# Merged tiles of a graph kernel: source one-hots of four windows by one 512-element comparison

## The chip, the cores and the metric

The kernel runs on one core of a Trainium2 chip. The metric is the device time of one execution in microseconds (us). A core has a matmul engine (TensorE, "PE" in the profile, its weight loads "PEld"), a vector engine (VectorE, "DVE"), an activation engine (ScalarE, "ACT"), GpSimd ("POOL") and SyncE ("SP"), which issues DMAs. Each engine works through its own instruction list and waits on semaphores.

## The reference

Two graph layers over 12,500 nodes of 64 features and 400,000 edges sorted by destination, each followed by a residual sum and a layer normalisation:

```python
# layer 0
gauss = exp(sum(-0.5 * (attr[:, None] - mu) ** 2 / (EPS + sigma ** 2), -1))      # E x 3
msg   = einsum('eko,ek->eo', (x[src] @ g).reshape(E, 3, 64), gauss)
out   = segment_sum(msg, dst) / max(cnt, 1) + x @ root_w + bias
x     = layernorm(x + silu(out + x))
# layer 1, twice a mean over neighbours
h = relu(x @ W_self1 + mean_of(x[src], dst) @ W_neigh1 + b1)
x = layernorm(x + h @ W_self2 + mean_of(h[src], dst) @ W_neigh2 + b2)
```

The two means of layer 1 are computed as dense products with a matrix of counts: how many edges run from node a to node b.

## The kernel before

Nodes lie in 98 tiles of 128. The kernel has five stretches: preparation of tables; a loop over the 98 tiles ("the tile loop"); a short check of the counts; layer 0's output; and the two dense products with the count matrix.

One turn of the tile loop does two things that share the engines.

**Counts.** For one tile of destinations it builds its 128 x 12,544 block of the count matrix in 32 windows of four destinations. Each window is a matmul of a source one-hot (128 edges x 128, which of 128 places within a tile of nodes the source has, the stationary operand) with a companion one-hot (128 edges x 392, which of 98 tiles and which of the window's four nodes, plus four columns of ones, the moving operand). Windows go in units of two: `n` = 0 to 15 is the unit, `w` = 0, 1 the window in it, `j = 2 * n + w`. VectorE writes the one-hots into a ring in SBUF (the tile `rE` in the trace), raises `a_pair` once per unit; TensorE waits for it, multiplies into PSUM (`pu`, three pairs of banks, `pw` in the trace) and raises `a_used`; ScalarE copies the unit's counts out (line 584), and raises `a_evac`. VectorE may write a ring place again only when `a_used` has passed the unit that read it.

There are three kinds of tile. A *paired* tile takes one or two pairs of edge batches per window; VectorE writes two interleaved source one-hots by one `tensor_tensor` of 256 elements (line 1281) and two companions by `tensor_scalar` (line 1283). A *merged* tile has all its window's edges in one batch of 128; per window VectorE writes one source one-hot (line 1410, `tensor_scalar`, 128 elements, the key from `parts[:, 1, j]`, one value per partition) and one companion (line 1411, `tensor_scalar`, 392 elements). The order is: two first tiles, then 40 tiles in which 26 merged and 14 paired tiles (two pairs per window) alternate, as merged, paired, merged; then 32 paired tiles (one pair per window); then 24 merged tiles. So there are 50 merged tiles and 1,600 instructions of line 1410.

**Messages.** For the same turn's 4,096 edges, POOL gathers the source rows by 32 indirect DMAs (line 498), into a buffer of two turns; ScalarE (line 545) and VectorE (line 1326) scale them by the three weights; per chunk `u` of four, VectorE compares destinations (lines 1340 and 1343), TensorE multiplies (line 809, eight f32 matmuls per destination tile that the chunk touches) and VectorE adds the sums (line 1263). In VectorE's list, `prepare` of chunk u stands behind unit 4u + 1; in TensorE's list, `chunk` does too. POOL may gather into a part of its buffer when ScalarE (`a_wg`) and VectorE (`a_wgd`) are done with it, and ends each turn with a wait for its own last gathers.

At the start of a merged tile VectorE copies the 64 integer keys `parts_i` to f32 `parts` (line 1399), loads its table words into registers (line 1316) and goes on with unit 0. After unit 1 it works off what is left of the previous tile (`listed`, lines 1268, 1276, 1474, 1439).

Of the kernel before, what the change touches and what calls it, by code (L numbers as in the profile page):

```python
# [7 lines left out]
F16 = mybir.dt.float16  # L8
BF16 = mybir.dt.bfloat16
ALU = mybir.AluOpType  # L10
# [3 lines left out]
P = 128  # L14
# [9 lines left out]
JW = P // W  # L24
NU = JW // 2
RU = 4
# [5 lines left out]
CW = HP * W  # L32
# [33 lines left out]
def gnn_kernel(nc, x, src, dst, attr, g, mu, sigma, root_w, bias, w_self1, w_neigh1, b1,  # L66
# [18 lines left out]
    with ExitStack() as ctx:  # L85
        def sb(name, shape, dt=F32):
            return ctx.enter_context(nc.sbuf_tensor(name, shape, dt))
# [8 lines left out]
        rE = sb("rE", [P, RE])  # L96
# [9 lines left out]
        comp = rE[:, o:o + RU * 4 * CW // 2].bitcast(F16).rearrange("p (r b c) -> p r b c", r=2 * RU, b=2)  # L106
        o_lo = o + RU * 4 * CW // 2
        lo1h = rE[:, o_lo:o_lo + RU * 4 * P // 2].bitcast(F16).rearrange("p (r c b) -> p r c b", r=2 * RU, b=2)
        lo_flat = rE[:, o_lo:o_lo + RU * 4 * P // 2].bitcast(F16).rearrange("p (r w c) -> p r w c", r=2 * RU, w=2)
        assert o_lo + RU * 4 * P // 2 <= RE  # L110
        o_src = 2 * KB * D
        o_dst = o
# [66 lines left out]
        consts = sb("consts", [P, 4, K * A])  # L179
        iota = sb("iota", [P, P])  # L180
        iota_2 = sb("iota_2", [P, P, 2], F16)
        iota_h = sb("iota_h", [P, P], F16)
        iperm = sb("iperm", [P, GW], F16)
        pidx = sb("pidx", [P, 1])
        ident = sb("ident", [P, P])
# [32 lines left out]
        both, behind2, merged_i, parts_i, parts = sca, bmx, winw, wi, wf  # L218
# [5 lines left out]
        pu = [pw[0], pw[1], pw[3]]  # L224
# [478 lines left out]
        def _(pe):  # L703
# [117 lines left out]
            def unit(t, n, pairs_w):  # L821

                evacuated(t, n)
                pe.wait_ge(a_pair, t * NU + (n + 1))
                for w in range(2):
                    if pairs_w == 0:
                        r = 2 * n % (2 * RU)
                        ins = pe.matmul(pu[n % 3][:, w, 0:CW], lo_flat[:, r, w, :], comp[:, r, w, :], start=True, stop=True)  # L828
                        if n % (NU // U) == 2 and w == 0:
                            ins.then_inc(a_chunk, 1)  # L830
                    for p in range(pairs_w):
                        r = ((2 * n + w) * pairs_w + p) % (2 * RU)
                        for b in range(2):
                            ins = pe.matmul(pu[n % 3][:, w, 0:CW], lo1h[:, r, :, b], comp[:, r, b, :],  # L834
                                            start=(p == b == 0), stop=(p == pairs_w - 1 and b == 1))
                            if n % (NU // U) == 2 and w == p == b == 0:
                                ins.then_inc(a_chunk, 1)
                ins.then_inc(a_used, 1)
# [75 lines left out]
            for part, (base, n) in enumerate(PARTS):  # L914
                with pe.Fori(0, tiles[n], 1):
                    pe.wait_ge(f_tab, pe.snap(fixed, min_val=16, max_val=16 * NT + 16))
                    pe.sem_inc(s_tick[0], 1)
                    with pe.Fori(0, wins, 1) as c:
                        w = nc.s_assert_within(pe.snap(c - wins + JW, min_val=0, max_val=JW - 1), 0, JW - 1,
                                               skip_runtime_bounds_check_because="the last windows of a tile")  # L920
# [91 lines left out]
        def _(dve):  # L1012
# [7 lines left out]
            V = nc.vector  # L1020
# [74 lines left out]
            behind = scan(rowa, rowb, NT, slice(0, 1))  # L1095
# [43 lines left out]
            for c in range(2):  # L1139
                V.tensor_copy(sca[0:NT, c, :], pb[6 + c][0:NT, 0:JW])  # L1140
                ins = V.tensor_copy(hist[0:NT, c, :], pb[6 + c][0:NT, 0:JW])
# [81 lines left out]
                    evacuate(dve, n, s_evv)  # L1223

            dve.wait_ge(s_tabw, 1)
            V.tensor_copy(iota_h[:], iota[:])
            V.tensor_scalar(win_p[:], iota[:, 0:JW], float(GW * P), None, ALU.mult)
            V.memset(comp[:].rearrange("p r b c -> p (r b) c")[:, :, GW:CW], 1.0)
            V.memset(gr[:], -1.0e6)
# [164 lines left out]
            def merged_counts(q, t, s=None, behind=2, following=None):  # L1394

                other = slot_of(q + 1) if s is None else 1 - s
                s = slot_of(q) if s is None else s
                dve.wait_ge(a_pair, q * NU)
                V.tensor_copy(parts[:], parts_i[:]).then_inc(a_hand, 1)
                words_of(q, s)  # L1400
                dve.wait_ge(a_hand, q + (1 - DT))
                for u in range(U):
                    for n in range(u * NU // U, (u + 1) * NU // U):

                        free = n + 1 if behind < 2 else max(n + 1, min(n + 3, 4))
                        dve.wait_ge(a_used, q * NU + free)
                        r = 2 * n % (2 * RU)
                        for w in range(2):
                            j = 2 * n + w
                            V.tensor_scalar(lo_flat[:, r, w, :], iota_h[:], parts[:, 1, j:j + 1], None, ALU.is_equal)  # L1410
                            ins = V.tensor_scalar(comp[:, r, w, 0:GW], iperm[:], parts[:, 0, j:j + 1], None, ALU.is_equal)  # L1411
                        ins.then_inc(a_pair, 1)
                        if n == 1:

                            listed(q - 1, other)
                            base_of(q, t)
                        if n % (NU // U) == 1:
                            prepare(q, s, u)
                        if following is not None:
                            merge_between(n, q, following, other)  # L1420
                for k in range(2):
                    dve.reg_mov(xw[k], words[T_X + k])
                dve.reg_mov(xn, words[T_XT])
# [357 lines left out]
```

## Time and profile before

| what | us |
|---|---|
| median of three runs | 8616.2 |
| lowest, highest | 8571.03, 8632.65 |
| span of the profiled execution, first to last instruction | 7138.9 |
| PE busy in it | 4916.9 (69%) |
| DVE busy | 4364.6 (61%) |
| POOL busy | 3409.5 (48%) |
| ACT busy | 2701.0 (38%) |

The page gives no other time for the profiled execution than its span. The three runs lie 1432 to 1494 us above that span: this is time outside the first and last instruction of the program, which the trace does not show. Busy time counts instructions of the engines and not those of their sequencers (register loads, waits). On VectorE consecutive instructions overlap: an instruction starts before the one ahead of it ends, so that a mean duration is longer than the time the instruction takes from its list.

### The profile page before, as it was taken

To read this page: it belongs to the slowest core of one execution; us is meant where nothing else is said; L and a number is where in the kernel's file an instruction comes from. 1 tells how busy PE (TensorE), PEld (TensorE's weight loads), DVE (VectorE), ACT (ScalarE), POOL (GpSimd) and SP (SyncE) were. 2 spreads that over 40 slices of the span, in tenths; PEclk is the share of its full clock that TensorE was granted. 3 is DMA by queue.
4 is the path that set the end of the run, shared out by engine and by line. 5 is a ranking of instruction groups with operands and counts; after the bars stand their busy time and mean duration, and the time that the engine had idled before them with its cause. 6 is when DMAs were issued, how large, how long until landed. Compare 5 with 4: busy or idle time off the path is not lost.

```text
span 7138.9 us, 141917 instructions
## 1 busy us (share of the span) xinstructions
PE 4916.9 (69%) x35195; PEld 3933.0 (55%) x35196; DVE 4364.6 (61%) x15089; ACT 2701.0 (38%) x8318; POOL 3409.5 (48%) x3146
## 2 busy tenths in 40 slices
PE   1466666666666655566666665565647999999999
PEld 1123444444444433444444444444437999999999
DVE  5667787777777776777777766666645222222222
ACT  3112554554555543455554455555532000000000
POOL 5013776677766665677777777777720000000000
PEclk5556888888888887788888878888867999999999
DMA  3001222222222222222222222222234999999998
GB/s 77 30 25 48 92 83 92 82 97 97 78 95 78 96 78 72 94 96 96 95 77 96 95 97 87 91 94 97 96 92 157 382 380 383 380 368 385 384 385 341
DMA packets 258332, 1082.60 MB, mean 152 GB/s; under 512 B 140102, under 2 KB 144230, under 8 KB 194406
## 3 DMA queue, kind: packets, MB, share of 16 engines
q1 hardware_dynamic: 139588, 965.46, 34.6%
q0 software_dynamic: 100352, 102.96, 6.4%
q10 hardware_dynamic: 18120, 11.31, 0.7%
q8 instruction: 78, 1.28, 0.1%
q14 instruction: 194, 1.59, 0.1%
HBM read 751.67 MB, written 327.81 MB: 151 GB/s over the span
## 4 chain that ended last, share of the span: by engine, by line
PE 39%; DVE 19%; issue 14%; POOL 11%; DVEq 10%; ACT 4%; DMA 2%; ACTq 0%; SPq 0%; POOLq 0%
PE pw L983 22%; POOL rE L498 11%; PE pw L809 9%; DVE rE L1283 5%; PE pw L834 3%; DVEq L1316 3%; DVEq L1492 2%; DVE rE L1343 2%; PE pw L781 2%; DVE rE L1281 2%; ACT rE L545 2%; DVE rE L1411 1%; ACT rB L584 1%; DMA rE<-in_x,idx 1%; DVEq L1268 1%
## 5 line engine op out<-in xcount | busy, mean ns | idle before, releaser
L498 POOL DMA_INDIRECT rE<-in_x,idx x3136 | 3407.4, 1087 | 1828.5 <-issue 1745.6
L809 PE MATMUL pw<-rE 128*128 128x193 f32 x7824 | 1688.3, 377 | 863.1 <-DVE rE L1343 810.2
L584 ACT CAST rB<-pw 128x792 bf16<-128x792 f32 x1568 | 1257.2, 813 | 2509.8 <-PE pw L834 1151.1
L809 PEld LDWEIGHTS pw<-rE 128*128 128x128 f32 x7824 | 1539.5, 222 | 1064.5 <-DVE rE L1343 985.5
L545 ACT ACTIVATE rE<-rE,cols 128x64 f32<-128x64 f32 x4704 | 1255.4, 345 | 8.1 <-DMA tab<-tab_d 8.1
L834 PE MATMUL pw<-rE 128*128 128x396 f16 x3840 | 809.8, 358 | 487.1 <-DVE rE L1283 440.6
L1283 DVE TENSOR_SCALAR rE<-iperm,gr 128x392 f16<-128x392 f16 x3840 | 1051.3, 313 | 0.1
L834 PEld LDWEIGHTS pw<-rE 128*128 128x128 f16 x3840 | 370.1, 103 | 865.9 <-DVE rE L1283 532.0
L983 PE MATMUL pw<-rB,rA 128*128 128x192 bf16 x9604 | 810.7, 246 | 0.1
L983 PE MATMUL pw<-rE,rA 128*128 128x192 bf16 x9604 | 810.5, 246 | 0.1
L983 PEld LDWEIGHTS pw<-rB,rA 128*128 128x128 bf16 x9604 | 790.7, 98 | 1.6
L983 PEld LDWEIGHTS pw<-rE,rA 128*128 128x128 bf16 x9604 | 790.5, 98 | 1.6 <-issue 0.2
L678 ACT COPY gcol<-pw 128x128 f32<-128x128 f32 x196 | 52.0, 265 | 1492.5 <-PE pw L991 1491.5
L828 PE MATMUL pw<-rE 128*128 128x396 f16 x1600 | 375.7, 353 | 329.8 <-ACT rB L584 182.2
L1343 DVE TENSOR_TENSOR rE<-iota,local 128x1024 f32<-128x1024 f32 x489 | 592.5, 1212 | 0.0
L1281 DVE TENSOR_TENSOR rE<-iota,lr 128x256 f16<-128x256 f16 x1920 | 539.2, 281 | 68.2 <-PE pw L834 24.0
L1411 DVE TENSOR_SCALAR rE<-iperm,wf 128x392 f16<-128x392 f16 x1600 | 541.0, 338 | 0.0
L1410 DVE TENSOR_SCALAR rE<-iota_h,wf 128x128 f16<-128x128 f16 x1600 | 398.3, 249 | 177.4 <-issue 149.2
L781 PE MATMUL pw<-rE 128*128 x822 | 305.9, 477 | 224.4 <-DVE rE L1276 132.6
L1263 DVE TENSOR_TENSOR rA<-pw,rA 128x193 f32 x491 | 172.4, 351 | 410.1 <-PE pw L809 409.2
L828 PEld LDWEIGHTS pw<-rE 128*128 128x128 f16 x1600 | 135.4, 99 | 510.8 <-DVE rE L1411 244.2
L1326 DVE TENSOR_TENSOR rE<-rE,cols 128x768 f32 (+1 forms) x392 | 371.4, 947 | 54.7 <-DVE wbase L1434 43.2
(258 smaller groups left out, 2550.8 us busy)
## 6 DMA issues: line engine op xcount, KB each, us to landing
rA<-count SPq DMA_DIRECT2D x392, 1568.0 KB, 8.4
count<-rB SPq DMA_DIRECT2D x98, 3136.0 KB
rE<-in_x,idx POOLq DMA_INDIRECT x3136
cols<-cols_d SPq DMA_DIRECT2D x98, 64.0 KB
cols_d<-rA SPq DMA_DIRECT2D x3, 1568.0 KB, 5.2
rA<-in_edge_attr ACTq DMA_DIRECT2D x1, 4608.0 KB
out<-gcol ACTq DMA_DIRECT2D x97, 32.0 KB, 5.7
count<-rB SPq DMA_DIRECT2D x8, 224.0 KB, 2.0
```

The source lines that it names most:

```text
L498: pool.indirect_dma_start(out=gath[:, s, u * CB + b, :], out_offset=None, in_=x, in_offset=bass.IndirectOffsetOnAxis(ap=idx[:, s, u * CB + ...
L545: ins = act.activation(wgath[:, u % 2, b, k * D:(k + 1) * D], gath[:, s, bb, :], ACT.Copy, scale=cols[:, s, 1 + k, bb:bb + 1])
L584: act.copy(stage[:, s, :, j * 2 * W:(j + 1) * 2 * W].rearrange("p h (w n) -> p w h n", w=2), pu[j % 3][:, :, 0:CW].rearrange("p w (h n) -> ...
L781: ins = pe.matmul(bank[:, 0:CW], lo1h[:, bass.ds(r, 1), :, b].rearrange("p o c -> p (o c)"), comp[:, bass.ds(r, 1), b, :].rearrange("p o c ...
L809: ins = pe.matmul(sums[side][:, 0:AW], onehot[:, side, bb, :], wgath[:, side, bb, :], start=(bb == 0), stop=(bb == CB - 1))
L828: ins = pe.matmul(pu[n % 3][:, w, 0:CW], lo_flat[:, r, w, :], comp[:, r, w, :], start=True, stop=True)
L834: ins = pe.matmul(pu[n % 3][:, w, 0:CW], lo1h[:, r, :, b], comp[:, r, b, :], start=(p == b == 0), stop=(p == pairs_w - 1 and b == 1))
L983: ins = pe.matmul(pb[s][:, 0:TW], ring[:, s, hi, :], table[:, hi].rearrange("p c d -> p (c d)"), start=False, stop=False, skip_group_check ...
L1281: V.tensor_tensor(lo1h[:, r], iota_2[:], lr[:, None, bass.ds(even, 2)].broadcast_to([P, P, 2]), ALU.is_equal)
L1283: ins = V.tensor_scalar(comp[:, r, h, 0:GW], iperm[:], float(GW * j), gr[:, bass.ds(at + h, 1)], ALU.add, ALU.is_equal)
L1343: V.tensor_tensor(onehot[:, side], iota[:, None, :].broadcast_to([P, CB, P]), local[:, :, None].broadcast_to([P, CB, P]), ALU.is_equal).th ...
L1411: ins = V.tensor_scalar(comp[:, r, w, 0:GW], iperm[:], parts[:, 0, j:j + 1], None, ALU.is_equal)
```

## The change

The source one-hots of two units, that is four windows or sixteen nodes, are written by one `tensor_tensor` comparison of 512 elements instead of four `tensor_scalar` of 128. Its first operand is a constant ramp `iota_4`, each number four times; its second is `lo_key`, the f16 keys of four windows, repeated 128 times. The four one-hots then lie interleaved, and TensorE reads its stationary operand with a step of four elements instead of one. A copy of 32 keys to f16 at the start of each merged tile is added. Since the comparison of an even unit writes the places of the next unit too, an even unit waits for one more unit of TensorE.

```diff
-        lo_flat = rE[:, o_lo:o_lo + RU * 4 * P // 2].bitcast(F16).rearrange("p (r w c) -> p r w c", r=2 * RU, w=2)
+        lo_four = rE[:, o_lo:o_lo + RU * 4 * P // 2].bitcast(F16).rearrange("p (h r c w) -> p h r c w", h=2, r=2, w=4)
...
-        iota_h = sb("iota_h", [P, P], F16)
+        iota_4 = sb("iota_4", [P, P, 4], F16)
+        lo_key = sb("lo_key", [P, JW], F16)
...
-                        ins = pe.matmul(pu[n % 3][:, w, 0:CW], lo_flat[:, r, w, :], comp[:, r, w, :], start=True, stop=True)
+                        ins = pe.matmul(pu[n % 3][:, w, 0:CW], lo_four[:, r // 4, 0, :, n % 2 * 2 + w], comp[:, r, w, :], start=True, stop=True)
...
-            V.tensor_copy(iota_h[:], iota[:])
+            V.tensor_copy(iota_4[:], iota[:, :, None].broadcast_to([P, P, 4]))
...
+                V.tensor_copy(lo_key[:], parts_i[:, 1, :])
                 V.tensor_copy(parts[:], parts_i[:]).then_inc(a_hand, 1)
...
-                        free = n + 1 if behind < 2 else max(n + 1, min(n + 3, 4))
+                        free = n + 2 - n % 2 if behind < 2 else max(n + 2 - n % 2, min(n + 3, 4))
                         dve.wait_ge(a_used, q * NU + free)
                         r = 2 * n % (2 * RU)
+                        if n % 2 == 0:
+                            V.tensor_tensor(lo_four[:, r // 4, 0], iota_4[:],
+                                            lo_key[:, None, 2 * n:2 * n + 4].broadcast_to([P, P, 4]), ALU.is_equal)
                         for w in range(2):
                             j = 2 * n + w
-                            V.tensor_scalar(lo_flat[:, r, w, :], iota_h[:], parts[:, 1, j:j + 1], None, ALU.is_equal)
                             ins = V.tensor_scalar(comp[:, r, w, 0:GW], iperm[:], parts[:, 0, j:j + 1], None, ALU.is_equal)
                         ins.then_inc(a_pair, 1)
```

VectorE's list at the start of a merged tile, before the change: the key copy (`wf` is `parts`, `wi` is `parts_i`), the load of the table words, and units 0 and 1.

```order
L1399 CAST wf<-wi 128x64
L1314 ISA
L1316 TENSOR_LOAD tab
L1401 REGISTER_ALU
L1406 REGISTER_ALU
L1410 TENSOR_SCALAR rE<-iota_h,wf 128x128
L1411 TENSOR_SCALAR rE<-iperm,wf 128x392
L1410 TENSOR_SCALAR rE<-iota_h,wf 128x128
L1411 TENSOR_SCALAR rE<-iperm,wf 128x392
L1406 REGISTER_ALU
```

The same place after the change, units 0 and 1 in full:

```order
L1400 CAST lo_key<-wi 128x32
L1401 CAST wf<-wi 128x64
L1315 ISA
L1317 TENSOR_LOAD tab
L1403 REGISTER_ALU
L1408 REGISTER_ALU
L1411 TENSOR_TENSOR rE<-iota,lo_key 128x512
L1415 TENSOR_SCALAR rE<-iperm,wf 128x392 x2
L1408 REGISTER_ALU
L1415 TENSOR_SCALAR rE<-iperm,wf 128x392 x2
```

For two units there were eight comparisons, and there are five; the piece of before shows the first four of the eight. Nothing else moves on any engine, and TensorE's list has the same instructions as before.

## Rows read from the trace of the kernel before

**Rows 1.** Busy time by stretch: stretch, its length, busy us of each engine with its count
```profile
core 0: us, PE busy (x) PEld busy (x) DVE busy (x) ACT busy (x) POOL busy (x), PEclk, DMA share, GB/s
...
620.00:2610.00 1990.00, 1227.41 (x5875) 844.80 (x5873) 1547.54 (x5632) 1037.41 (x3389) 1364.06 (x1270) 0.86 0.26 88
2610.00:4160.00 1550.00, 973.75 (x4605) 688.03 (x4605) 1166.31 (x4046) 755.39 (x2085) 1096.67 (x990) 0.81 0.26 89
4160.00:5270.00 1110.00, 667.61 (x3041) 507.80 (x3040) 720.04 (x2403) 639.11 (x2260) 788.10 (x749) 0.82 0.29 93
```

**Rows 2.** Chain that ended last, shares by line, stretches 620:2780 and then 4160:5270
```profile
by line: issue 18.1%; PE pw L809 14.8%; DVE rE L1283 10.5%; PE pw L834 6.9%; DVE rE L1281 4.8%; DVEq L1316 4.2%; DVE rE L1411 4.0%; DVEq L1492 4.0%; ACT rE L545 3.4%; DVE rE L1343 3.4%; DVE rE L1410 2.5%; ACT rB L584 2.4%; DVE rE L1326 2.0%
...
by line: POOL rE L498 50.4%; issue 23.3%; PE pw L809 7.5%; DMA rE<-in_x,idx 4.1%; ACT rE L545 1.7%; DVE rE L1343 1.6%; DVEq L1316 1.5%; PE pw L828 1.2%; DVE rE L1411 1.2%; ACT rB L584 1.1%; DVE rE L1410 0.9%; ACT sca L561 0.6%; DVE rE L1326
```

**Rows 3.** POOL's gathers: stretches 2610:4160, 4160:5270 (busy us, mean ns | idle before, releasers)
```profile
L498 POOL DMA_INDIRECT rE<-in_x,idx x990 | 1096.8, 1108 | 453.6 <-issue 429.8 <-ACT rE L545 16.8 <-DVE rE L1326 6.9
...
L498 POOL DMA_INDIRECT rE<-in_x,idx x749 | 788.1, 1052 | 290.9 <-issue 284.9 <-ACT rE L545 6.0
```

**Rows 4.** Timeline of POOL in a merged tile: start us, us, instruction [idle before]
```profile
4222.24 0.94 POOL L498 DMA_INDIRECT rE<-in_x,idx  x1 [0.30 <-issue]
4223.49 1.02 POOL L498 DMA_INDIRECT rE<-in_x,idx  x1 [0.30 <-issue]
4227.71 1.01 POOL L498 DMA_INDIRECT rE<-in_x,idx  x1 [3.20 <-issue]
```

**Rows 5.** Timeline of DVE, merged tile at 4217
```profile
4217.36 0.23 DVE L1410 TENSOR_SCALAR rE<-iota_h,wf 128x128 f16<-128x128 f16 x1
4217.52 0.31 DVE L1411 TENSOR_SCALAR rE<-iperm,wf 128x392 f16<-128x392 f16 x1
4217.75 0.24 DVE L1410 TENSOR_SCALAR rE<-iota_h,wf 128x128 f16<-128x128 f16 x1
4217.91 0.31 DVE L1411 TENSOR_SCALAR rE<-iperm,wf 128x392 f16<-128x392 f16 x1
4218.14 0.24 DVE L1410 TENSOR_SCALAR rE<-iota_h,wf 128x128 f16<-128x128 f16 x1
```

**Rows 6.** Timeline of DVE: `tensor_tensor` of 1024 f32 and 256 f16 elements, paired tile
```profile
3998.82 1.21 DVE L1343 TENSOR_TENSOR rE<-iota,local 128x1024 f32<-128x1024 f32 x1
3999.95 0.28 DVE L1281 TENSOR_TENSOR rE<-iota,lr 128x256 f16<-128x256 f16 x1
4000.15 0.54 DVE L1283 TENSOR_SCALAR rE<-iperm,gr 128x392 f16<-128x392 f16 x2
4000.62 0.28 DVE L1281 TENSOR_TENSOR rE<-iota,lr 128x256 f16<-128x256 f16 x1
```

**Rows 7.** DVE's groups on the page: busy, mean ns | idle before, releaser
```profile
L1410 DVE TENSOR_SCALAR rE<-iota_h,wf 128x128 f16<-128x128 f16 x1600 | 398.3, 249 | 177.4 <-issue 149.2
```

**Rows 8.** DVE's waits in 987:2569: us in total, times, longest us
```profile
DVE rA L1263 <- PE pw L809: 123.9, 29, 8.4
DVE rE L1410 <- issue: 60.6, 16, 5.0
DVE rB L1474 <- ACT rB L584: 30.4, 18, 2.6
DVE rB L1474 <- PE pw L781: 19.8, 14, 2.3
DVE rE L1281 <- PE pw L834: 19.7, 12, 3.7
...
DVE rE L1410 <- PE pw L828: 4.7, 5, 1.7
```

**Rows 9.** Weight loads of merged and paired tiles: duration ns min/median/max, first and last start
```profile
L828 PEld LDWEIGHTS pw<-rE x1600: 95/97/152, 685.5 to 5262.2; 128*128 128x128 f16 x178
...
L834 PEld LDWEIGHTS pw<-rE x3840: 96/98/152, 627.4 to 4149.0; 128*128 128x128 f16 x192
```

**Rows 10.** Timeline of PE behind a string of four units
```profile
4218.03 1.17 PE L828 MATMUL pw<-rE 128*128 128x396 f16 x6
4219.52 0.51 PE L828 MATMUL pw<-rE 128*128 128x396 f16 x2 [0.31 <-ACT rB L584]
4221.18 0.59 PE L809 MATMUL pw<-rE 128*128 128x193 f32 x2 [1.15 <-DVE rE L1343]
```

## Prediction

> **What bounds the kernel now.** I first split the span by stretch [rows 1], then read the chain that ended last over the stretches that hold merged tiles [rows 2]. POOL issues 32 gathers per tile, so the counts of the first view give the tiles: 1270 / 32 = 40 tiles from 620 to 2610 us (26 merged, 14 paired), 990 / 32 = 31 from 2610 to 4160, 749 / 32 = 24 from 4160 to 5270. A tile takes 1990 / 40 = 49.8 us, 1550 / 32 = 48.4 us and 1110 / 24 = 46.3 us.
>
> In the last of these, the reader should see that the chain is POOL and its gaps: 50.4% and a part of the 23.3% "issue", while line 1410 has 0.9% [rows 2]. The timeline of POOL says why: a gather is followed by a gap of 0.30 us, and once per tile by 3.20 us for the gathers' own landing [rows 4]. With the mean of 1052 ns [rows 3], a tile needs 32 x (1.052 + 0.30) + 2.9 = 46.2 us. That is the whole 46.3 us: the 24 last merged tiles go at POOL's pace, and VectorE is busy for only 720 of 1110 us.
>
> In the mixed stretch, POOL by the same sum needs 32 x (1364.06 / 1270 + 0.30) + 2.9 = 46.9 us of the 49.8 us, so it has 2.9 us a tile to spare. POOL isn't among the lines of that chain; VectorE and TensorE alternate in it, VectorE with 1547.54 us busy of 1990 [rows 1, 2]. Only here, and in the last two tiles, when the gathers are over, can VectorE's time become kernel time.
>
> **The change part by part.** *What is removed.* A mean duration is not what an instruction costs, since they overlap; the distance of starts is. In a string of a merged tile, line 1411 starts 0.16 us after line 1410, and the next 1410 starts 0.23 us after 1411 [rows 5]. So a source one-hot takes 0.16 us of the list and not its mean 249 ns [rows 7]. Four of them take 0.65 us (4 x 0.162, as 0.39 us a window less 0.23).
>
> *What is added.* The trace has no 512-element f16 comparison. It has two neighbours: 1024 f32 elements take 1.13 us from start to start (3998.82 to 3999.95) and 256 f16 elements, broadcast in runs of two, take 0.20 us [rows 6]. With half the time per f16 element, 1024 s + f = 1.13 and 128 s + f = 0.20 give s = 1.04 ns and a fixed part f = 0.07 us; 512 f16 elements then take 0.33 us. The bound above, at the f32 pace, is 0.07 + 0.53 = 0.60 us. The bound below is the 0.20 us of the 256 elements. I take 0.33: the new operand is the form of line 1281 with runs of four in place of two.
>
> So two units save 0.65 - 0.33 = 0.31 us (bounds 0.05 and 0.45), a tile 8 x 0.31 = 2.5 us, 50 tiles 125 us of VectorE's list.
>
> The Trainium skill ("VectorE: DVE Perf Modes", the tier table and the table of errata-adjusted cycles) speaks against this change: `tensor_scalar` on 16-bit data runs at four elements a cycle, `tensor_tensor` at two, and both have the same fixed 58 cycles. By its figures, an estimate, four of 128 elements cost 375 ns and one of 512 costs 327 ns, which would leave 0.4 us a tile. The row disagrees on the first term: 0.16 us and not 94 ns. The measurement decides, and the small `tensor_scalar` is mostly fixed cost.
>
> *Which of it is on the path.* Mixed stretch: 26 x 2.5 = 65 us at most. The chain bounds it from the other side: line 1410 holds 2.5% of 2160 us = 54 us there and 0.9% of 1110 = 10 us later [rows 2]; of these 64 us the fraction 0.31 / 0.65 goes, 31 us. Between the two lies what other engines absorb: VectorE already waits for engines that don't wait for it, 30.4 + 19.8 + 19.7 + 4.7 = 75 us in 1582 us [rows 8], 2.3 us a tile, and when VectorE gets faster such a wait grows. The 123.9 us for line 809 are another matter: this TensorE work starts from VectorE's own line 1343 and moves with it. I take about two thirds of 65, 42 us. The last two tiles give 2 x 2.5 less a wait, 3 us.
>
> *The POOL-bound stretch.* Nothing of the 60 us saved on VectorE counts directly. But gathers are slower while VectorE works on its strings: undisturbed 0.94 us [rows 4], in the merged stretch 1052, in the paired one 1108 [rows 3]. The excess a tile is 32 x 0.11 = 3.5 us where the strings last 16 x 0.79 = 12.6 us, and 32 x 0.168 = 5.3 us where they last 32 x 0.67 = 21.4 us (the distance of two line 1281s in [rows 6]). The slope is 1.8 / 8.8 = 0.2 us per us; strings shorter by 2.5 us give back 0.5 us a tile, 12 us in 24 tiles. Bounds: 0 (the excess comes with the edges of strings, whose number stays), and 24 us (only `tensor_scalar` disturbs, of which 12.6 us become 7.4).
>
> *What I cost at nothing.* The copy to `lo_key` stands ahead of the table load, behind which VectorE's engine sits idle anyway, 149.2 us "issue" before line 1410 [rows 7]; uncovered it would be 50 x 0.2 = 10 us, some 5 of them on the path. The weight load with a step of four elements: with a step of two it takes 98 ns, with one 97 [rows 9], and PE's time beside it is longer; were it 0.1 us longer, the last unit's two loads before each chunk would show, 0.2 x 4 x 26 = 21 us. The longer wait of an even unit: unit 4u + 4 now needs unit 4u + 1, which in TensorE's list stands ahead of chunk u, while VectorE passes `prepare` of chunk u first. TensorE is done with its four units (4220.03) before it waits 1.15 us for line 1343 [rows 10], so the ring isn't full there. VectorE's wait for line 828 at line 1410 is 4.7 us in 32 tiles [rows 8]; doubled it costs 5 us. A pair of units is handed over no later: the even one after 0.33 + 0.46 = 0.79 us, as before, the odd one after 0.46 instead of 0.79.
>
> Sum: 42 + 3 + 12 = 57 us. Of the span it leaves 7138.9 - 57 = 7082 us. The time around the span is no part of the change, so I take the same 57 us off the median: 8616.2 - 57 = 8559 us.
>
> **The rivals.** *Absorbed* (0.25): the gain of the mixed stretch goes into waits for ScalarE's copy and for TensorE, and POOL's excess belongs to the edges of strings. For it: TensorE and ScalarE lines of the chain [rows 2] and the 2.3 us of waits a tile, nearly as much as the 2.5 us saved. Against it: VectorE is busy in 78% of the stretch. What stays is the chain's share and less, 0 to 31 us; middle 15, 8601 us.
>
> *POOL freed* (0.13): `tensor_scalar` alone holds POOL up, and all of VectorE's saving passes. 65 + 5 + 24 = 94 us, 8522 us. Against it stands the paired stretch, whose strings already hold a `tensor_tensor` in every group of three and have the longer gathers [rows 3, 6]. The Trainium skill ("SBUF — State Buffer", who interferes with whom) has the rule for this rival: a `tensor_scalar` in a two-port mode locks POOL out of the shared ports, a `tensor_tensor` takes only the read side, which descriptor writing doesn't need. No row separates the two here.
>
> *The comparison at one element per beat* (0.04): 0.60 us in place of 0.33. The saving falls to 0.4 us a tile, 7 us on the path and 2 at POOL: 8607 us, no change.
>
> *Slower* (0.04): gathers are held up more by strings in which 392-element comparisons follow each other four at a time. Its place is the POOL-bound stretch; each 10 ns per gather cost 24 x 32 x 0.01 = 7.7 us. It decides from (42 + 3) / 7.7 x 10 = 59 ns more than 1052, just over the paired stretch's 1108. With twice that distance, 112 ns, it costs 86 us: 8616 + 86 - 45 = 8657 us. A tile of the mixed stretch has 2.9 us of room for it.
>
> **How the numbers follow.** The forecast proper, 31 to 85 us saved, has 0.54. 8559 us is its middle. The range 8515 to 8612 takes in the forecast, the upper end of the freed POOL, and most of the absorbed case, and holds a little over 8 in 10. A change of 1% is 86 us, about what a measurement of this kernel can tell from none: the three runs lie 0.7% apart. Faster by over 1% needs most of the third case and the edge of the first: 0.13. Slower by over 1% is part of the last: 0.02. The rest, 0.85, is within 1%.
>
> **What would show it.** The new comparison should take 0.33 us from its start to the next one's. The stretch of 40 mixed tiles should last 1990 - 42 = 1948 us, with POOL's mean near 1070 there; the 24 last tiles 1110 - 15 = 1095 us, with gathers of 1037 ns. The paired stretch stays at 1550 us. The weight load of merged tiles stays under 110 ns. I am wrong in the path if the mixed stretch changes by less than 26 us while the comparison takes 0.33 us, and wrong on POOL if its mean in the last stretch rises, or falls below 1020 ns.

## The result, and the profile after

The changed kernel takes 8622.0 us (median of 20 runs, 8587 to 8680), the kernel before 8575.5 us in 20 runs beside it (8511 to 8633). The ratio is 1.0052, 95% interval 1.0032 to 1.0073: 0.5% slower. The prediction was 8559 us, 57 us or 0.7% below the 8616.2 us it started from; both the sign and the range missed. (That start, a median of three runs, lay 41 us above the median of twenty.) In the classes of the prediction, "within 1%" holds.

In the changed kernel line numbers are higher by one to four: 498 is 499, 809 is 810, 828 is 829, 834 is 835, 1283 is 1284, 1360 is 1361. The new comparison is line 1411, its companions are line 1415.

The changed kernel's page: the span, the queues that fetch instructions (packets, MB, share of 16 engines), and two groups (busy us, mean ns | idle us before, releaser).

```profile
span 8635.7 us, 140462 instructions
...
q14 instruction: 342, 2.80, 0.1%
q8 instruction: 78, 1.28, 0.1%
...
L499 POOL DMA_INDIRECT rE<-in_x,idx x3136 | 3242.0, 1034 | 3424.1 <-issue 3420.2
...
L1411 DVE TENSOR_TENSOR rE<-iota,lo_key 128x512 f16<-128x512 f16 x400 | 168.5, 421 | 335.0 <-remote 137.4
```

Its span is 8635.7 us and the kernel's time in the same execution 8637.5 us. So there are 2 us around the span. The kernel before had shown a span of 7138.9 us against a median of 8616.2 us. That this one execution was not like the timed ones came out when the kernel before was profiled again, unchanged:

```profile
span 8611.3 us, 141917 instructions
...
q8 instruction: 78, 1.28, 0.1%
q14 instruction: 194, 1.59, 0.1%
...
L498 POOL DMA_INDIRECT rE<-in_x,idx x3136 | 3247.1, 1035 | 3398.4 <-issue 3391.1
```

The 1477 us that I took to lie around the span lie inside it: the timed program takes 14 to 16 us more for every tile. From here on "before" means this second trace. Read beside that of after, it has one row of the page that is quite different: 194 packets of instructions on q14 against 342.

The weight loads and the new comparison of after, line by line (duration in ns min/median/max, first and last start; below the last, where VectorE waited in us and times):

```profile
L829 PEld LDWEIGHTS pw<-rE x1600: 110/113/152, 730.2 to 6762.7; 128*128 128x128 f16 x178
...
L835 PEld LDWEIGHTS pw<-rE x3840: 96/98/152, 668.1 to 5301.5; 128*128 128x128 f16 x192
...
L1411 DVE TENSOR_TENSOR rE<-iota,lo_key x400: 404/420/483, 729.2 to 6758.3; 128x512 f16<-128x512 f16 x134
...
  PE pw L829: 64.9, 56
```

VectorE's timeline of after in a merged tile (start us, us, instruction):

```profile
5503.86 0.42 DVE L1411 TENSOR_TENSOR rE<-iota,lo_key 128x512 f16<-128x512 f16 x1
5504.19 1.11 DVE L1415 TENSOR_SCALAR rE<-iperm,wf 128x392 f16<-128x392 f16 x4
5505.22 0.41 DVE L1411 TENSOR_TENSOR rE<-iota,lo_key 128x512 f16<-128x512 f16 x1
5505.56 1.10 DVE L1415 TENSOR_SCALAR rE<-iperm,wf 128x392 f16<-128x392 f16 x4
```

From start to start the comparison takes 0.33 us, as worked out. Over the 115 unbroken strings of four units in each trace, first start to last end, the shortest is 2.60 us where before (profiled again) it was 3.23, the mean 2.96 where it was 3.49. So VectorE's list did get shorter, by 0.5 to 0.6 us per four units, and the kernel longer.

Where the time is shows best by stage. I cut the spans where ScalarE's last copy of a tile ends: 34 mixed tiles, then the 32 paired ones, then the 24 last merged ones. First the kernel before (profiled again), then after; columns as in [rows 1].

```profile
1070.00:3229.00 2159.00, 1144.23 (x4934) 796.35 (x4932) 1291.56 (x4667) 894.84 (x2880) 1129.18 (x1088) 0.76 0.22 69
3229.00:5293.00 2064.00, 1045.62 (x4603) 747.11 (x4603) 1203.44 (x4034) 766.83 (x2080) 1057.78 (x1024) 0.73 0.21 67
5293.00:6745.00 1452.00, 713.95 (x3032) 554.27 (x3032) 712.79 (x2391) 649.85 (x2260) 714.89 (x704) 0.74 0.23 70
```

```profile
1070.00:3229.00 2159.00, 1150.90 (x4935) 826.60 (x4936) 1237.03 (x4142) 895.36 (x2880) 1115.77 (x1088) 0.76 0.23 69
3229.00:5312.00 2083.00, 1041.70 (x4603) 742.76 (x4601) 1210.20 (x4029) 766.45 (x2080) 1074.62 (x1024) 0.72 0.22 67
5312.00:6764.00 1452.00, 718.08 (x3032) 570.93 (x3032) 654.01 (x1842) 653.26 (x2260) 705.75 (x704) 0.74 0.23 70
```

The merged tiles, which the change touches, take the same time in both. The stretch that is longer, by 19 us, is that of the paired tiles, in which no statement was changed. One trace of each proves little: spans of one kernel differ by up to 60 us (8532.2 and 8592.1 us in the two runs of one kernel below). It did say where to look.

### The profile page after: what moved, and what is told of

Read it like the earlier page. It is cut to its first block, busy times and chain, and to the rows that moved or that the text cites. A ratio compares the mean times of both kernels' runs of the same rounds, so it can differ in the third digit from the quotient of the medians.

```text
span 8635.7 us, 140462 instructions
## 1 busy us (share of the span) xinstructions
PE 5178.6 (60%) x35195; PEld 4175.5 (48%) x35196; DVE 4293.3 (50%) x13939; ACT 2745.5 (32%) x8318; POOL 3244.2 (38%) x3146
## 4 chain that ended last, share of the span: by engine, by line
PE 36%; DVE 17%; another core or an unknown queue 14%; issue 14%; DVEq 11%; ACT 7%; ACTq 1%; DMA 1%; SPq 0%
PE pw L984 18%; PE pw L810 9%; DVE rE L1284 4%; PE pw L835 3%; ACT rE L546 3%; DVEq L1317 2%; DVE rE L1344 2%; ACT rB L585 2%; DVEq L1496 2%; DVE rE L1282 2%; PE pw L782 2%; PE pw L829 1%; DVEq L1284 1%; DVE rE L1415 1%
## 5 line engine op out<-in xcount | busy, mean ns | idle before, releaser
L499 POOL DMA_INDIRECT rE<-in_x,idx x3136 | 3242.0, 1034 | 3424.1 <-issue 3420.2
L810 PE MATMUL pw<-rE 128*128 128x193 f32 x7824 | 1885.1, 409 | 1123.4 <-DVE rE L1344 909.1
L810 PEld LDWEIGHTS pw<-rE 128*128 128x128 f32 x7824 | 1740.7, 247 | 1333.3 <-DVE rE L1344 1021.1
L835 PE MATMUL pw<-rE 128*128 128x396 f16 x3840 | 867.4, 377 | 1066.4 <-ACT rB L585 477.2
L1284 DVE TENSOR_SCALAR rE<-iperm,gr 128x392 f16<-128x392 f16 x3840 | 1076.2, 321 | 58.8 <-issue 56.2
L835 PEld LDWEIGHTS pw<-rE 128*128 128x128 f16 x3840 | 384.3, 107 | 1473.7 <-issue 780.2
L829 PE MATMUL pw<-rE 128*128 128x396 f16 x1600 | 389.5, 366 | 684.0 <-ACT rB L585 351.1
L829 PEld LDWEIGHTS pw<-rE 128*128 128x128 f16 x1600 | 166.0, 119 | 844.6 <-issue 501.5
L1415 DVE TENSOR_SCALAR rE<-iperm,wf 128x392 f16<-128x392 f16 x1600 | 430.0, 328 | 9.5 <-remote 8.2
L1411 DVE TENSOR_TENSOR rE<-iota,lo_key 128x512 f16<-128x512 f16 x400 | 168.5, 421 | 335.0 <-remote 137.4
```

The costliest lines, as they stand in the source:

```text
L499: pool.indirect_dma_start(out=gath[:, s, u * CB + b, :], out_offset=None, in_=x, in_offset=bass.IndirectOffsetOnAxis(ap=idx[:, s, u * CB + ...
L810: ins = pe.matmul(sums[side][:, 0:AW], onehot[:, side, bb, :], wgath[:, side, bb, :], start=(bb == 0), stop=(bb == CB - 1))
L829: ins = pe.matmul(pu[n % 3][:, w, 0:CW], lo_four[:, r // 4, 0, :, n % 2 * 2 + w], comp[:, r, w, :], start=True, stop=True)
L1284: ins = V.tensor_scalar(comp[:, r, h, 0:GW], iperm[:], float(GW * j), gr[:, bass.ds(at + h, 1)], ALU.add, ALU.is_equal)
```

## The experiments

There are eighteen runs, of fifteen kernels. All ratios are against runs of the kernel before on the same chip, with 95% intervals.

**First group: the parts of the change, one by one.** Both kernels unchanged again:

> The kernel before, unchanged, for a trace that can be set beside that of the changed kernel: the timed executions of before last 8511 to 8633 us, but the profiled one only 7139 us, so the trace on which the forecast rests is of an execution that the timed ones did not resemble. If the extra time of the changed kernel's trace (its span is 8636 us) belongs to every normal execution, this trace shows it too: span 8510 to 8630 us, tiles of about 60 us in the last 24 and not 46.3, POOL's idle time near 3400 us and not 1828.5. If it belongs to the change, the span is 7139 us again. The ratio to before is 1.000 within 0.3%, which also says what a comparison can resolve.

> The changed kernel, unchanged, on the chip on which the others of this batch run: 1.003 to 1.007 of before by the 20 runs so far. The other runs are read against this one.

Measured: before 1.0000 [0.9969, 1.0031], after 1.0038 [1.0012, 1.0064]. The slowdown stands.

The coarser wait alone, in the kernel before:

```diff
-                        free = n + 1 if behind < 2 else max(n + 1, min(n + 3, 4))
+                        free = n + 2 - n % 2 if behind < 2 else max(n + 2 - n % 2, min(n + 3, 4))
```

> The kernel before with one part of the change alone: an even unit of a merged tile waits for one more unit of TensorE. Theory A (the coarser wait costs the time: at the first comparison of a pair VectorE waits 56 times for line 829, 64.9 us, where it waited 10 times, 17.6 us, for line 828): 1.004 to 1.007, VectorE's waits at line 1410 for line 828 rise to some 60 us. Theory B (the weight load with a step of four costs it: 113 ns median against 97) and theory C (neither; the change's gain is lost elsewhere): 1.000 within 0.2%.

Measured: 1.0007 [0.9981, 1.0033]. The step-four read taken away from the changed kernel (its counts are then not the reference's):

```diff
-                        ins = pe.matmul(pu[n % 3][:, w, 0:CW], lo_four[:, r // 4, 0, :, n % 2 * 2 + w], comp[:, r, w, :], start=True, stop=True)
+                        ins = pe.matmul(pu[n % 3][:, w, 0:CW], lo_four[:, r // 4, 0, (n % 2 * 2 + w) * 32:(n % 2 * 2 + w) * 32 + 32, :].rearrange("p c w -> p (c w)"), comp[:, r, w, :], start=True, stop=True)
```

> The changed kernel, but TensorE reads its stationary operand of merged tiles densely (128 neighbouring elements of the same 512) instead of with a step of four; the counts are not the reference's. Theory B (weight load): the load is back at 97 ns and the time returns to before or below it, 0.993 to 1.000, since VectorE's saving is left. Theory A (ring wait) and theory C: as the changed kernel, 1.003 to 1.007; at most 3200 loads x 16 ns = 51 us could come back, and most of them lie beside matmuls, so 0 to 10 us.

Measured: 1.0039 [1.0015, 1.0063], as after. The load itself becomes shorter, 98 ns for 113, and nothing follows from it:

```profile
L829 PEld LDWEIGHTS pw<-rE x1600: 95/98/152, 735.7 to 6751.6; 128*128 128x128 f16 x178
```

The changed kernel with its one-hots spread over four quarters of the ring, so that the old wait does:

```diff
-                        ins = pe.matmul(pu[n % 3][:, w, 0:CW], lo_four[:, r // 4, 0, :, n % 2 * 2 + w], comp[:, r, w, :], start=True, stop=True)
+                        ins = pe.matmul(pu[n % 3][:, w, 0:CW], lo_four[:, n // 4 % 2, n // 2 % 2, :, n % 2 * 2 + w], comp[:, r, w, :], start=True, stop=True)
...
-                        free = n + 2 - n % 2 if behind < 2 else max(n + 2 - n % 2, min(n + 3, 4))
+                        free = n + 1 if behind < 2 else max(n + 1, min(n + 3, 4))
...
-                            V.tensor_tensor(lo_four[:, r // 4, 0], iota_4[:],
+                            V.tensor_tensor(lo_four[:, n // 4 % 2, n // 2 % 2], iota_4[:],
```

> The changed kernel, with the source one-hots of a pair of units spread over all four quarters of their memory instead of two of them, so that the comparison needs no longer wait than before (an even unit waits for the unit that it waited for before the change). Theory A (the coarser wait costs the time, now that VectorE is faster and meets it: 56 waits, 64.9 us): 0.997 to 1.001 of before, and VectorE's waits for line 829 at the 512-element comparison fall from 65 us to under 25 us. Theory D (what VectorE gains in its strings is lost again behind them, whatever the ring): 1.003 to 1.006, as the changed kernel.

Measured: 0.9998 [0.9971, 1.0024]. The loss is gone, which looked like a verdict on the wait. But the wait alone had cost nothing, and VectorE's waits for line 829 fell from 64.9 us to 45.4 only, where theory A wanted under 25, so that reading does not close.

The extra copy alone, then the order of the changed kernel with the old comparisons (and the coarser wait), then no source one-hots at all (counts not the reference's), each in the kernel before:

```diff
+                V.tensor_copy(lo_key[:], parts_i[:, 1, :])
```

> The kernel before with the added copy of 32 keys alone, which nothing reads. Costed at nothing, since it stands ahead of the load of the table words; uncovered it is 50 x 0.2 = 10 us. Every theory: 1.000 to 1.001.

```diff
+                        if n % 2 == 0:
+                            for k in range(4):
+                                V.tensor_scalar(lo_flat[:, r + k // 2 * 2, k % 2, :], iota_h[:], parts[:, 1, 2 * n + k:2 * n + k + 1], None, ALU.is_equal)
...
-                            V.tensor_scalar(lo_flat[:, r, w, :], iota_h[:], parts[:, 1, j:j + 1], None, ALU.is_equal)
```

> The kernel before with the order and the wait of the change, but with the old instructions: the four source one-hots of two units stand together ahead of the four companions, as four comparisons of 128 elements. The first unit of a pair is handed over 0.65 + 0.46 = 1.11 us after the start instead of 0.79, the second 0.46 us later. Theory E (the hand-over in pairs costs the time, as TensorE and ScalarE get their units in lumps): 1.004 to 1.010. Theories A and D: 1.000 to 1.003.

```diff
-                            V.tensor_scalar(lo_flat[:, r, w, :], iota_h[:], parts[:, 1, j:j + 1], None, ALU.is_equal)
```

> The kernel before without the source one-hots of merged tiles: all 1600 comparisons of 128 elements are left out and nothing is put in their place, so that the counts are wrong. 1600 x 0.16 = 259 us leave VectorE's list, twice what the change takes. By the forecast's path (two thirds in the mixed stretch, little in the last one): 2/3 x 133 + some 25 us at POOL = 115 us, 0.985 to 0.989. Theory D (in the timed executions VectorE's list isn't the bound; the gain is lost behind the strings): 0.996 to 1.002.

Measured: copy 1.0012 [0.9991, 1.0034]; order 1.0078 [1.0051, 1.0104]; no one-hots 1.0058 [1.0033, 1.0083]. The last one is the telling one. A kernel with 1600 fewer comparisons and nothing added was slower. No theory about strings, hand-overs or waits for the merged one-hots explains that well, and of all rows of the page one went with it: the packets on q14, 194, 195 and 187 in three kernels at 1.000 to 1.001 (before, copy, four quarters), and 342 to 348 in the others, of which all but one, the wait alone at 1.0007, are slower.

**The table that gave the new theory.** By stage, the extra packets lie in the paired stretch alone: 7 or 8 there in one set of kernels, 162 or 163 in the other, for 32 rounds of one loop. Its code for VectorE is 345 instructions long, and then the branch that closes it, in the compiled program of every kernel. What differs is where it starts, because the merged tiles' code ahead of it has a different number of instructions (the coarser wait removes 31 of them in all, 24 ahead of this loop). TensorE, ScalarE, POOL and SyncE have the same number of instructions in all of these kernels. A packet is 8 KB (2.80 MB / 342). With 128 instructions to a packet the starts, taken modulo 128, fall into two sets:

| kernel | start | mod 128 | q14 packets | ratio |
|---|---|---|---|---|
| before | 4439 | 87 | 194 | 1.0000 |
| copy alone | 4445 | 93 | 195 | 1.0012 |
| after, four quarters | 4301 | 77 | 187 | 0.9998 |
| coarser wait alone | 4415 | 63 | 348 | 1.0007 |
| order and wait | 4415 | 63 | 348 | 1.0078 |
| after | 4277 | 53 | 342 | 1.0052, 1.0038 |
| no one-hots | 4247 | 23 | 342 | 1.0058 |

A loop of 345 and its branch lies in three pieces of 128 for 39 of the 128 starts, and in four for the rest. Where a piece begins is fitted and not measured: counted from the kernel's own first instruction the 39 starts would have remainders 0 to 38, and to take in 77 to 93 and leave out 63 the pieces must begin at a remainder of 64 to 77. Pieces of 256 would not sort these starts at any offset. The theory: in three pieces the loop stays where VectorE reads its instructions, in four it is fetched anew in every round, and VectorE waits for it. The Trainium skill ("Perfetto Trace Analysis", The 4-stage abstract model) says that an instruction has 64 bytes, which gives, as an estimate, 8192 / 64 = 128 to a packet; the table agrees. The coarser wait at 1.0007 spoke against the theory and is taken up below.

**Second group: moving the loop.** Increments of a semaphore that nobody waits for stand just ahead of the loop. They move all of VectorE's code behind it as well, so "nothing else differs" in the expectation is too strong; but in these runs the q14 packets differ by more than one in the paired stretch alone:

```diff
+            for _ in range(40):
+                dve.sem_inc(s_tick[3], 1)
             with dve.Fori(0, QM - QC, 1) as i:
                 tile_counts(i + QC, i + T4, 1)
```

> The kernel before with 40 semaphore increments of VectorE, on a semaphore that nobody waits for, put just ahead of its loop over the 32 paired tiles; nothing else differs, and no merged tile behaves otherwise. It asks whether the place of that loop's code alone costs what the change cost. Counted in VectorE instructions from the program's start, the loop is 345 long and starts at 4439 in the kernel before, 4445 and 4301 in the two other kernels with 194 or fewer packets of instructions on q14, and at 4415, 4247 and 4277 in those with 342 to 348. One 8 KB packet being a run of instructions of a fixed number, 128 is the number for which these starts fall into two clean groups (remainders 77 to 93 with few packets, 23 to 63 with many): the loop then lies in three packets or in four. Here the remainder is about 126, so by the placement theory the loop lies in four: about 345 packets on q14, some 160 of them while the paired tiles run, the 32 paired tiles at 2077 to 2117 us in place of 2040 to 2064, and a ratio of 1.003 to 1.006. The rival, by which the time was lost in the merged tiles (the coarser wait, the hand-over behind a string), expects 194 packets or, if more, no time from them: 1.000 to 1.001. If both packets and time stay as before, the placement theory falls.

> The control to the run with 40: the same increments at the same place, 128 of them (127 compiled), so that the loop over the paired tiles starts at remainder 86 again, where it was in the kernel before. Placement theory: about 194 packets on q14, paired tiles 2040 to 2064 us, ratio 1.000 to 1.001 (128 increments at about 0.05 us are some 6 us of VectorE's time once, where it has slack). A theory by which the increments themselves cost time expects three times what the run with 40 costs: 1.009 or more if that one is at 1.003. The theory of the merged tiles expects 1.000 to 1.001.

Measured on one chip: with 40, 1.0086 [1.0063, 1.0109]; with 128, 1.0005 [0.9977, 1.0034]. Forty idle increments ahead of a loop cost 0.9%, and 128 nothing that can be seen. Their q14 rows, 40 first:

```profile
q14 instruction: 349, 2.86, 0.1%
```

```profile
q14 instruction: 195, 1.60, 0.1%
```

The queues in 132 us of the paired stretch, 3900 to 4032 us, of the kernel with 40 (columns as on the page); the same view of the kernel with 128 has no row for q14.

```profile
q1 hardware_dynamic: 1636, 6.59, 12.6%
q0 software_dynamic: 2343, 2.41, 9.2%
q14 instruction: 11, 0.09, 0.2%
```

And where VectorE stands for it. Line 1360 is among the first that VectorE computes in a round of the loop; the rows of the paired stretch give its idle time before them, 32 rounds each, for 40 and for 128:

```profile
L1360 DVE COPY lr<-locol 128x40 bf16 x64 | 10.6, 193 | 211.6 <-issue 211.6
```

```profile
L1360 DVE COPY lr<-locol 128x40 bf16 x64 | 10.6, 197 | 155.1 <-issue 154.9
```

57 us more, at one place. The sequencer's records name it: behind the branch that closes the loop, the next instruction comes after 2.8 us (median of 32 rounds) with 40 increments, after 0.25 us with 128. The paired stretch of the two traces lasts 2104 and 2059 us.

The other direction, in the changed kernel:

> The changed kernel with 32 such increments just ahead of the loop over the paired tiles, which brings its start from remainder 53 to 84. Everything that the change does in the merged tiles is left as it is. Placement theory: q14 falls from 342 to about 187 packets, the 32 paired tiles from 2083 to 2104 us back to 2040 to 2064, and the ratio from 1.0052 to 0.998 to 1.001. Theory of the merged tiles (the coarser wait and the string that hands over later): packets may fall but the ratio stays at 1.003 to 1.006. If it comes out below 0.998, the predicted gain was there and was covered by the placement.

Measured: 0.9969 [0.9951, 0.9988], 187 packets, paired stretch 2048 us. The same comparison row for after and for after with 32 increments:

```profile
L1361 DVE COPY lr<-locol 128x40 bf16 x62 | 10.3, 201 | 211.5 <-issue 211.5
```

```profile
L1361 DVE COPY lr<-locol 128x40 bf16 x62 | 10.3, 200 | 137.1 <-issue 137.1
```

So the whole loss of the change, and a little more, was the place of code that it doesn't touch. In this comparison the version is faster than both kernels; a near twin below comes to 0.9982.

The order alone, with the old wait and thus the old place:

> The kernel before with only the order of its merged strings changed as in the changed kernel: the one-hots of two half-words are made ahead of the companions, four at a time, in a ring of four quarters, with the old wait and the old number of instructions (5764), so the paired loop stays where it was (remainder 87). The run with this order and the coarser wait gave 1.0078, at remainder 63 and 348 packets. Placement theory alone: 194 packets and 1.000 to 1.002, since the placement was the cost of that run. Order theory (the first four one-hots stand ahead of the first companion, so TensorE gets its first string 0.5 us later in each merged half-word pair): 194 packets too, but 1.003 to 1.005, which with the placement adds up to the 1.0078.

Measured: 1.0013 [0.9988, 1.0038], 194 packets. With the old wait no cost of the order can be seen. The run at 1.0078 is not explained by its place alone, though: the wait alone, in the same place, gave 1.0007 and gives 1.0026 below. In the good place the order and the coarser wait ran together only with the new comparison (0.9969, 0.9982), so those 0.5 to 0.7% stay open.

**Third group: what is left of the gain, and whose it is.** The coarser wait once more, then with 25 increments that bring the loop back to 4439:

> The kernel before with the coarser wait alone, a second time. Its paired loop lies in the costly place (start 4415, remainder 63; 348 packets on q14). If placement costs 0.7 to 0.9% everywhere and the coarser wait nothing, the ratio is 1.006 to 1.009 and the first 1.0007 was a stray; if the coarser wait itself brings 0.6%, it is 1.000 to 1.002 again.

> The same with increments ahead of the paired loop that bring its start back to 4439, remainder 87, where it is in the kernel before: about 194 packets. Coarser wait worth nothing: 0.999 to 1.001. Coarser wait a gain of its own: 0.992 to 0.996, and then the changed kernel's gain in the good place would be the wait's.

Measured: 1.0026 [1.0007, 1.0046] in the costly place, 0.9972 [0.9947, 0.9998] in the good one. The place costs this kernel too, 0.5% by this pair on one chip and 0.3% by the earlier 1.0007, which may be the sum of that cost and of a small gain. No one-hots, and after with 33 increments:

> The kernel before without the one-hot comparisons of the merged tiles (they are left out, so its counts are not those of the reference), with the paired loop brought to start 4309, remainder 85. In the costly place this kernel measured 1.0058. It gives the most that any cheaper comparison could bring. By the prediction's shares (2.5 us of VectorE's list saved per merged tile gave 57 us; here 5.2 us are saved per tile) it would be 0.987 to 0.990; if the string behind and its hand-over take the place of the comparison, as the traces of the changed kernel suggest, 0.996 to 0.999.

> The changed kernel in the good place, looked at a second time with one increment more than before (start 4309, remainder 85, 187 packets on q14). If the 0.9969 stands, 0.995 to 0.999; if the change brings nothing in the good place and the first look was a stray, 0.999 to 1.001.

Measured: 0.9944 [0.9922, 0.9966] (its counts aren't the reference's) and 0.9982 [0.9962, 1.0003]. The last pair, on one chip:

> The kernel before with the coarser wait alone and its paired loop in the good place (start 4439), a second look beside the other run of this pair. If the wait is what gains, 0.995 to 0.999 again; if the first 0.9972 was a stray, 0.999 to 1.002.

> The comparison of 512 elements with the old, finer wait (ring of four quarters, start 4301, 187 packets), a second look. If the comparison brings nothing and the wait is what gains, 0.999 to 1.002, above the other run of this pair by 0.3%; if the comparison gains what the prediction gave it, 0.993 to 0.997, no higher than the other.

Measured: 0.9980 [0.9955, 1.0005] and 0.9982 [0.9961, 1.0003]. In the good place there are then: the change as it is 0.9969 and 0.9982, the wait alone 0.9972 and 0.9980, the comparison without the wait 0.9998 and 0.9982. The comparison can't be told from the wait, and neither is far from nothing; whose the 0.2% is stays open. By stage the traces show no gain of the new comparison either: with the stages of the two traces above, its four traces in the good place have a mean of 2159 us in the mixed stretch and 1456 in the last, the six there with the old comparison 2159 and 1446.

Over all profiled kernels, whatever was done to their merged tiles, the stages read as follows (mean us, with the standard error of the mean):

| | mixed, 34 tiles | paired, 32 | last, 24 |
|---|---|---|---|
| loop in three pieces, 11 traces | 2160 ± 4 | 2059 ± 4 | 1446 ± 5 |
| loop in four pieces, 8 traces | 2168 ± 5 | 2092 ± 5 | 1435 ± 10 |

33 us, 0.4%, in the one stretch. The pairs that differ by the place alone differ by 0.3 to 1.1% in time (0.8% before, 0.6 to 0.8% after, 0.3 to 0.5% with the wait alone, 1.1% without one-hots), some 25 to 100 us. The whole spans of these traces differ by 26 us in the mean (8628 ± 11 and 8601 ± 8). The part above 33 us I could not place: the first and last stages differ by about their errors or less. One trace goes against the row, the kernel without one-hots in the good place, at 2087 us in the paired stretch.

## Why the prediction was wrong

**The comparison: right.** 0.33 us from start to start, forecast 0.33. By the Trainium skill ("VectorE: DVE Perf Modes", the table of errata-adjusted cycles) an estimate gives 327 ns; the trace agrees. The saving is there, or nearly: 0.5 us (means) to 0.6 us (shortest strings) per four units, four times a tile, is 2.1 to 2.5 us per merged tile, forecast 2.5.

**Costed at nothing, and nearly right:** the copy (1.0012, interval around one), the step of four (113 ns and not under 110 as I said, without effect: 1.0039 with and without), the order (1.0013). The longer wait: VectorE waits 64.9 us for line 829 before line 1411 where the profile of before gave 17.6 us at line 1410 and its repetition 23.0, and the runs of the wait alone in the good place (0.9972, 0.9980), with 31.2 us of such waits in the first, show no cost. The order is cleared only with the old wait; with the coarser one 0.5 to 0.7% stay unexplained.

**Costed at nothing, and wrong: the code that the change removes.** "The longer wait of an even unit" was treated as a wait only. It also removes instructions, as the larger comparison does, and so shifts all code of VectorE that follows. This step wasn't in the working at all. It is worth 0.6 to 0.8% here, 50 to 70 us, about as much as the whole forecast of 57, and it decided the sign. The rival on the slower side, longer gathers, was not what happened: their mean in the last stage fell from 1015 to 1002 ns (714.89 / 704 and 705.75 / 704), close to the 15 ns I had given, and no time came of it: the last stretch is 1452 us in both. (The sign "wrong on POOL if it falls below 1020 ns" says nothing here, since before, profiled again, is below it already.)

**"The time around the span is no part of the change": false premise.** I took the one traced execution as a picture of the timed ones although it was 1477 us shorter. In the timed ones POOL's idle time is 3398 us, not 1828. In the last stage it is 650 us of 1452, where by [rows 3] it was 291 of 1110. The waits are at the start of chunks; POOL's timeline of before, profiled again, has in one tile

```profile
5719.19 1.13 POOL L498 DMA_INDIRECT rE<-in_x,idx  x1 [13.13 <-issue]
...
5745.19 0.96 POOL L498 DMA_INDIRECT rE<-in_x,idx  x1 [5.13 <-issue]
```

where [rows 4] has one gap of 3.20 us. So "the 24 last merged tiles go at POOL's pace" fails for the execution that is timed, and with it the 12 us from freed gathers. The two traces without one-hots say the same. Their last stretch is 1406 us in the good place and 1382 in the costly one, 40 to 53 us under the means of the table, while their mixed stretch is no shorter (2173 and 2174 us). The prediction had said of the mixed stretch that "only here", and in the last two tiles, can VectorE's time become kernel time; by these two traces it is the other way round, and their paired stretch is 25 to 28 us longer than the means (2087 and 2117 us).

**The share of VectorE's time that reaches the path: mis-sized.** The prediction's own sign of this came: the mixed stretch did not change (34 tiles in 2159 us, before and after) while the comparison took its 0.33 us. I took 57 of 125 us, 46%. Taking the source one-hots out altogether, 0.65 x 8 = 5.2 us a tile or 260 us of VectorE's list, in the good place gave 0.56% = 48 us, 18% (six runs; the interval is 29 to 67 us). At 18% the change's 125 us are worth 23 us; measured were 15 to 27 us (0.9982 and 0.9969), with intervals from nothing to 42 us. The rival "absorbed" (0 to 31 us, middle 15) had the right size for this part. VectorE's waits name the reason: in the last stage of before (profiled again) it stands 412 us in front of one line, for TensorE and for causes outside the trace ("remote").

```profile
L1410 DVE TENSOR_SCALAR rE<-iota_h,wf 128x128 f16<-128x128 f16 x766 | 192.9, 252 | 150.1 <-issue 80.0 <-remote 60.0 <-PE pw L828 7.0
...
L1263 DVE TENSOR_TENSOR rA<-pw,rA 128x193 f32 x137 | 48.5, 354 | 412.3 <-remote 227.3 <-PE pw L809 94.5 <-issue 90.5
```

A string that ends 0.6 us earlier only starts these waits earlier. That the waits as such took the gain is argued from these rows; shown is only the size, by the kernel without one-hots.

## What to carry to other kernels

If an edit adds or removes instructions, compare the counts of instruction packets on the page before and after, and look in the stretches that the edit does not touch; a loop whose code just fits can be pushed over an edge, and idle increments ahead of it push it back. How many are needed has to be tried, since the place of the edge was fitted here and not known. Judge a small edit against a version in which such a loop lies in the same place, or its 0.2% drowns in 0.8% of placement. And hold the span of the profiled execution against the timed median first: where they differ by more than a few us, a bound read from the trace may not be that of the timed runs, and a second profile is worth more than a second argument.

## What the runs showed of the hardware

- A loop of VectorE of 345 instructions stays in place when it lies in three pieces of 128 and is fetched again in every round when it lies in four: 163 packets of 8 KB in 32 rounds, five a round, against 7 or 8 in all. The packets are measured; that the pieces are of 128 instructions rests on ten different starts falling into two sets.
- The jump back costs VectorE 2.8 us where the code comes again (40 increments), and 0.25 us where it does not (128).
- The timed executions have pauses that the first trace lacks. In the kernel before, profiled again, VectorE and TensorE stand still together while POOL goes on issuing gathers. VectorE's timeline, TensorE's, and of POOL's one row in the same 18 us:

```profile
5985.40 0.43 DVE L1340 TENSOR_SCALAR local<-cols,tile 128x8 f32 x1 [0.39 <-DVE rE L1343]
6003.84 0.36 DVE L1263 TENSOR_TENSOR rA<-pw,rA 128x193 f32 x1 [18.02 <-remote]
```

```profile
6005.39 1.01 PE L809 MATMUL pw<-rE 128*128 128x193 f32 x2 [16.72 <-DVE rE L1343]
```

```profile
5992.38 0.94 POOL L498 DMA_INDIRECT rE<-in_x,idx  x1 [0.30 <-issue]
```

  Some 400 to 500 of the sequencer's operations of VectorE take 0.70 us each in such traces, none in the first one. The gap between the two kinds of execution is 1470 us, 30 times what was studied here. What causes it wasn't tried and stays open.
